# Post-norm decoder: who forms the norms' epsilon, bias and rows, and the masked queries

## The reference

```python
m = mean(x); v = var(x)                       # _layernorm
x = (x - m) / sqrt(v + 1e-5)

x = ln(x + nystrom_attention(x))              # 16 heads, 64 landmarks, 6 pseudo-inverse steps
x = ln(x + dilated_attention(x, ctx, ctx))    # 16 heads, three branches, causal
x = ln(x + ternary_ffn(x))                    # 256 -> 1024 -> 256, gelu
x = ln(x + memory_attention(x))               # 4 heads, decayed and causal
x = ln(x + gated_attention(x, ctx, ctx))      # 8 heads, rope; has a norm of its own inside
x = ln(x + experts(x))                        # 8 experts, top 2
```

## Time and profile before

| | before |
|---|---|
| median of 3 runs | 1829.68 us (1816.7 to 1835.09) |
| the profiled execution's own time | 1817.69 us |
| its span | 1815.6 us |
| mean granted PE clock | 0.90 |
| PE busy | 1408.0 us, 78% |
| PE weight loads busy | 1161.9 us, 64% |
| DVE (VectorE) busy | 1055.8 us, 58% |
| ACT (ScalarE) busy | 628.7 us, 35% |
| POOL (GpSimd) busy | 370.1 us, 20% |

### The profile page before, as it was taken

The page is one execution under the profiler, slowest core; times in us unless marked ns, Lnnn a source line. Parts: engine busy times, 40 slices in busy tenths (PEclk is TensorE's granted clock), DMA queues, the critical chain, the costliest instruction groups (busy, mean ns, idle before and its releaser), DMA issues. The chain is left out here.

```text
span 1815.6 us, 46593 instructions
## 1 busy us (share of the span) xinstructions
PE 1408.0 (78%) x19740; PEld 1161.9 (64%) x19740; DVE 1055.8 (58%) x2385; ACT 628.7 (35%) x1371; POOL 370.1 (20%) x374
## 2 busy tenths in 40 slices
PE   1798886799788679988777988866405999999960
PEld 0696664479577359866546966644404888888860
DVE  4577568567666676766857675684132444444425
ACT  1322543432353434243443314533102434443420
POOL 0013132211314121211511121421342000000016
PEclk9798998989999799999888989989657999999985
DMA  6111122211211123100413201201244766677723
GB/s 262 37 50 36 49 58 79 74 49 38 59 29 44 49 76 107 44 13 2 116 53 100 62 25 49 82 1 42 68 147 142 254 221 217 216 235 243 228 76 119
DMA packets 165449, 174.80 MB, mean 96 GB/s; under 512 B 10528, under 2 KB 130208, under 8 KB 164896
## 3 DMA queue, kind: packets, MB, share of 16 engines
q1 hardware_dynamic: 154688, 154.33, 26.9%
q10 hardware_dynamic: 7520, 9.58, 1.5%
q0 software_dynamic: 3072, 8.39, 1.4%
HBM read 126.39 MB, written 45.88 MB: 95 GB/s over the span
## 5 line engine op out<-in xcount | busy, mean ns | idle before, releaser
L2092 PE MATMUL m_bank<-e_xT,e_w 128*128 128x256 bf16 x2208 | 246.2, 274 | 0.5 <-DVE e_xT L2170 0.5
L2092 PEld LDWEIGHTS m_bank<-e_xT,e_w 128*128 128x128 bf16 x2208 | 216.7, 98 | 26.7 <-DVE e_xT L2170 0.9
L684 PE MATMUL bank<-arena 64*64 64x64 f32 (+2 forms) x6400 | 219.0, 227 | 8.4 <-DVE arena L869 3.5
L684 PEld LDWEIGHTS bank<-arena 64*64 64x64 f32 x6400 | 213.5, 138 | 16.7 <-issue 6.2
L1724 POOL TENSOR_TENSOR e_parts<-e_whole,e_parts 128x512 bf16<-128x512 f32 x96 | 112.6, 1178 | 512.0 <-ACT e_parts L1718 512.0
L2183 DVE TENSOR_TENSOR e_h<-m_bank,e_silu 128x256 f32<-128x256 f32 x184 | 78.2, 425 | 202.6 <-ACT e_silu L2135 202.6
L2104 PE MATMUL m_bank<-m_xT,e_h 128*128 128x256 bf16 x1104 | 124.1, 273 | 0.0
L2104 PEld LDWEIGHTS m_bank<-m_xT,e_h 128*128 128x128 bf16 x1104 | 108.0, 98 | 12.3
L2135 ACT ACTIVATE e_silu<-m_bank 128x256 f32<-128x256 f32 x184 | 70.5, 383 | 124.8 <-PE m_bank L2092 124.8
L1541 DVE TENSOR_REDUCE arena<-bank 128x1 f32<-128x512 f32 x128 | 79.8, 683 | 28.7 <-PE bank L1452 28.4
L1609 ACT ACTIVATE arena<-bank 128x512 f32<-128x512 f32 x128 | 66.5, 604 | 82.9 <-PE bank L1477 82.8
(11 more groups left out here) (295 smaller groups left out, 2721.9 us busy)
## 6 DMA issues: line engine op xcount, KB each, us to landing
e_w<-parts SPq DMA_DIRECT2D x92, 512.0 KB, 5.4
e_whole<-E SPq DMA_DIRECT2D x96, 256.0 KB, 3.1
parts<-e_parts SPq DMA_DIRECT2D x192, 128.0 KB, 2.9
m_xT<-parts SPq DMA_DIRECT2D x46, 512.0 KB, 8.0
slots<-zeros SPq DMA_DIRECT2D x4, 1536.0 KB, 7.5
back<-e_y ACTq DMA_DIRECT2D x23, 256.0 KB, 6.5
e_x<-slots SPq DMA_DIRECT2D x22, 256.0 KB, 6.7
w_rest<-W_rest SPq DMA_DIRECT2D x1, 3584.0 KB, 25.0
```

What stands on the lines that cost most here:

```text
L684: last = pe.matmul(b[r, p * width:(p + 1) * width], lhs[r, 4 * g + p, :], rhs[r, 4 * g + p, :], start=True, stop=True)
L2092: last = pe.matmul(bank[b][:, col:col + SLOTS], w[:, wp, c, f * P:(f + 1) * P], xeT[u][:, xp, c, :], start=j == 0, stop=j == len(terms) - 1)
```

## The change

ScalarE writes the normalised rows, as an activation with a scale (the reciprocal standard deviation) and a bias; VectorE forms only that bias, −mean × rstd, two columns; GpSimd adds the epsilon ahead of the power. ScalarE also forms the masked queries, from a bias that the setup has multiplied by the parity once. The tables of all five engines' orders are written anew.

```diff
-        def dve_norm(dve, bat, link, key, src, dst):
+        def dve_norm(dve, bat, link, key, src):
...
             for t in range(NT):
                 last = dve.bn_aggr(v["mv"][:, t, :], v["st"][:, t, :])
-            link(last)
-            dve.tensor_scalar(v["ve"][:], v["mv"][:, :, 1], EPS, None, ALU.add).then_inc(sem(f"variance{key}_{s}"), 1)
+            last.then_inc(sem(f"variance{key}_{s}"), 1)
             yield
             dve.wait_ge(sem(f"rstd{key}_{s}"), due("rstd", bat, 1))
+            dve.scalar_tensor_tensor(v["shift"][:], v["mv"][:, :, 0], -1.0, v["rstd"][:], ALU.mult, ALU.mult)\
+                .then_inc(sem(f"shift{key}_{s}"), 1)
+
+        def act_normalize(act, bat, key, src, dst):
+            s, v = bat % STREAMS, st[bat]
+            act.wait_ge(sem(f"shift{key}_{s}"), due("shift", bat, 1))
             for t in range(NT):
-                last = dve.tensor_scalar(dst[:, t, :], src[:, t, :], v["mv"][:, t, 0:1], v["rstd"][:, t:t + 1],
-                                         ALU.subtract, ALU.mult)
+                last = act.activation(dst[:, t, :], src[:, t, :], ACT.Identity, bias=v["shift"][:, t:t + 1],
+                                      scale=v["rstd"][:, t:t + 1])
             last.then_inc(sem(f"x{key}_{s}"), 1)
...
         def pool_norm(pool, bat, key):
             s, v = bat % STREAMS, st[bat]
             pool.wait_ge(sem(f"variance{key}_{s}"), due("variance", bat, 1))
+            pool.tensor_tensor(out=v["ve"][:], in0=v["mv"][:, :, 1], in1=EPSC[:], op=ALU.add).then_inc(sem(f"above{key}_{s}"), 1)
+            pool.wait_ge(sem(f"above{key}_{s}"), due("variance", bat, 1))
             pool.tensor_tensor(out=v["rstd"][:], in0=v["ve"][:], in1=NEGH[:], op=ALU.pow)\
                 .then_inc(sem(f"rstd{key}_{s}"), 1)
...
+                for u in range(2):
+                    link(dve.tensor_scalar(dq_masked[:, NC * u:NC * (u + 1)], bias["dq"], consts["parity"][:, u:u + 1], None, ALU.mult))
...
-            b = bk.await_filled(dve, "d_q")
+            b = bk.await_filled(act, "d_q")
             for u in range(2):
                 for m in range(NC):
-                    last = dve.tensor_scalar(n["qm"][:, u, m, :], b[:, m * T:(m + 1) * T], bias["dq"][:, m:m + 1],
-                                             consts["parity"][:, u:u + 1], ALU.add, ALU.mult)
+                    last = act.activation(n["qm"][:, u, m, :], b[:, m * T:(m + 1) * T], ACT.Identity,
+                                          bias=dq_masked[:, 2 * u + m:2 * u + m + 1], scale=consts["parity"][:, u:u + 1])
             last.then_inc(bk.emptied("d_q"), 1)
...
 ORDERS = {
-    "pe": """0x2 1x2 0x1 1x2 0x1 1x1 0x1 1x2 0x2 1x2 0x1 1x1 0x1 1x8 0x1 1x6 0x8 1x5 0x18 1x24 0x12 1x7 0x2 1x32 0x1 1x7 0x9 1x2
+    "pe": """1x2 0x2 1x2 0x1 1x1 0x2 1x2 0x2 1x2 0x1 1x1 0x1 1x8 0x1 1x5 0x2 1x25 0x6 1x4 0x23 1x40 0x3 1x2 0x13 1x6 0x3 1x1 0x12
```

More of the change, by code:

```diff
@@ L188 @@
+    1x4 2x1 0x1 2x1 0x3 2x6 1x2 2x1 1x1 0x2 2x1 0x1 2x6 1x3 0x1 1x1 0x1 2x1 1x2 0x1 2x1 0x1 1x4 2x1 0x2 2x1 0x3 2x1 0x1
+    2x2 1x1 2x2 1x3 2x1 0x4 2x7 1x2 2x1 1x1 0x1 2x1 0x1 2x1 0x1 2x5 1x2 2x2 1x1 0x1 1x1 0x1 2x1 0x2 1x4 0x1 1x2 0x5 2x4
+    1x1 0x1 2x1 1x1 0x1""",
+    "sp": """2x24 3x2 2x21 1x3 0x3 2x24 1x2 2x3 0x2 2x9 3x1 2x39 1x2 2x2 0x2 2x19 1x2 2x3 3x1 2x3 0x2 2x48 1x1 2x2 1x1 2x4 0x2 2x3
+    3x1 2x12 1x2 2x3 0x2 2x70 1x1 0x1""",
 }
-PER_BATCH = {"input_turned": 16, "input": 16, "context": 16, "stored": 16, "res": 5, "variance": 1, "rstd": 1, "x": 1,
+PER_BATCH = {"input_turned": 16, "input": 16, "context": 16, "stored": 16, "res": 5, "variance": 1, "rstd": 1, "shift": 1, "x": 1,
@@ L451, in layers_kernel @@
         NEGH = sb("neghalf", [P, NT])
+        EPSC = sb("epsilon", [P, NT])
+        dq_masked = sb("dq_masked", [P, 2 * NC])
         with nc.Block() as block:
@@ L477, in _ @@
                 pool.memset(NEGH[:], -0.5)
+                pool.memset(EPSC[:], EPS)
                 pool.memset(zeros[:], 0.0)
@@ L941, in act_nystrom @@
             yield
+            act_normalize(act, bat, "0", v["y"], v["x"])
+            yield
             act_norm(act, bat, "n_xT")
@@ L983, in dve_residual_norm @@
             bk.await_emptied(dve, name)
-            yield from dve_norm(dve, bat, link, key, v["y"], v["x"])
+            yield from dve_norm(dve, bat, link, key, v["y"])
         def pool_norm(pool, bat, key):
@@ L1143, in dve_dilated @@
             yield
-            b = bk.await_filled(dve, "d_q")
-            for u in range(2):
-                for m in range(NC):
-                    last = dve.tensor_scalar(n["qm"][:, u, m, :], b[:, m * T:(m + 1) * T], bias["dq"][:, m:m + 1],
-                                             consts["parity"][:, u:u + 1], ALU.add, ALU.mult)
-            last.then_inc(bk.emptied("d_q"), 1)
-            yield
             b = bk.await_filled(dve, "d_v")
@@ L1227, in act_dilated @@
             yield
+            b = bk.await_filled(act, "d_q")
+            for u in range(2):
+                for m in range(NC):
+                    last = act.activation(n["qm"][:, u, m, :], b[:, m * T:(m + 1) * T], ACT.Identity,
+                                          bias=dq_masked[:, 2 * u + m:2 * u + m + 1], scale=consts["parity"][:, u:u + 1])
+            last.then_inc(bk.emptied("d_q"), 1)
+            yield
             b = bk.await_filled(act, "d_k")
@@ L1562, in dve_gated @@
             bk.await_emptied(dve, "g_out")
-            yield from dve_norm(dve, bat, link, "4", n["u"], n["n"])
+            yield from dve_norm(dve, bat, link, "4", n["u"])
             yield
@@ L1572, in dve_gated @@
             yield
-            yield from dve_norm(dve, bat, link, "5", v["y"], v["y"])
+            yield from dve_norm(dve, bat, link, "5", v["y"])
         def act_gated(act, bat):
@@ L1611, in act_gated @@
             yield
+            act_normalize(act, bat, "4", n["u"], n["n"])
+            yield
             b = bk.await_filled(act, "g_nT")
```

98 lines of the change are left out of this document (51 added, 47 removed).

## The result

The changed kernel takes **1863.97 us** (median of 4, 1862.84 to 1868.64) against 1826.76 us (median of 4, 1816.7 to 1835.09) for the kernel before: a ratio of 1.0211, interval 1.0154 to 1.0268. It is about 38 us slower. The prediction was 1820 us, with a range of 1792 to 1850; both are missed on the slow side.

The account below looks back on a forecast made before the run. No engine was taken as full: two streams of dependent steps fill each other's gaps, and PE's waits count. −15 + 20 − 13 + 4, say −4 us, from 1823.7, halfway between two scales, gave 1820 us, range 1792 to 1850.

Parts of the forecast that it names:

- VectorE's relief: Layers: net 60 us less work on VectorE, of which a quarter reaches the end, −15 us (−5 and −30 kept).
- the prediction named 75: Layers: sign that PE's waits for VectorE outside norms fall from 97 to about 75 us; if they stay, relief worthless.
- The chain: Each norm, from PE's product to PE's transposes: 0.9 us longer, between +0.6 and +1.3, from 3.6 to 4.5 us.
- the bound for the add: GpSimd's two-column epsilon add in each norm: 0.4 us taken, between a memset's 0.10 and the power's 0.78.
- What the chain costs: The 40 norms that feed PE: 53 us not covered by the other stream's work with chain 4.5, +20 us.
- What the order gives back: Waits at lines 1122 and 1294: the new order hides most of one (−9) and half the other (−4), −13 us.
- The two named waits: PE at line 1122 for line 1197 (10.8 us in 8) and at 1294 for 1336 (8.6 in 8).
- ScalarE, +4 us: Layers: ScalarE gains 128 instructions, 72 us, of which 6% counts, as PE waits for it 6% of the time.
- The norm's chain becomes the bound: Rival, chance 0.22: feed-forward norms and stream 0's fourth, second and third pair; +25 us, about 1848.
- over 65 us of waits for the normalised x: Sign at PE's transposes: waits above about 65 us in all decide for the rival of the norm's chain as bound.
- Relief passes through: Rival, chance 0.30: VectorE bounds where ropes, row maxima and norms of both streams meet; −26 us, about 1798.
- nothing moves: Rival, chance 0.08: the order keeps PE's gaps as they are and both effects stay off PE, 1824 us.

Follow-up runs that it names:

- The queries: Kernel before with its old order, only the masked queries moved from VectorE to ScalarE: 1830.27 us, 1.0014.
- the new placement: The changed kernel's instructions under the five order tables of the kernel before (the old order): 1858.13 us, 1.0197.
- the second power: Kernel before, old order and placements, with one more GpSimd power into a spare tile ahead of each norm's power: 1856.44 us, 1.0166.
- The rows alone: Kernel before, old order, only the normalised rows moved to ScalarE, VectorE forming the bias: 1845.63 us, 1.0112.
- load added there: Kernel before with two more VectorE 128x256 instructions into a spare tile behind each norm's normalising pair, 96 in all: 1888.31 us, 1.0342.
- the old placement: The instructions of the kernel before, on their old engines, under the changed kernel's five order tables: 1853.03 us, 1.0169.
- the added load: Kernel before plus spare 128x256 instructions: 48 on ScalarE behind copies of norms' transposes (1827.41 us, 0.9995); the hardware note means 96 on VectorE behind norms (1888.31 us, 1.0342).

## Why the prediction was wrong, point by point

The sum was −15 + 20 − 13 + 4 = −4 us, and the measurement is +38. Three steps failed: the relief of VectorE and the order's gift did not come, and the sum had no term for PE being busy longer at a lower clock.

**VectorE's relief, −15 us: about nothing.** The queries' 15 us gave 1.0014, and the new placement with 47 us less VectorE work (808 to 761) costs no less than the second power, which relieves nothing. (The rows alone cost 10 us less than the second power at the same chain, but their intervals overlap, and the new placement with more relief does not bear it out.) The step that failed is "I take a quarter" of the removed work. PE's waits for VectorE outside norms stayed at 95.6 in the old order; the prediction named 75 and said that if they stay, the relief was worth nothing. At the one place read closely, the removed work stood where PE was itself held, in order, before the late rows; that this holds for all of it is argued and not shown. That load added there costs 62 us does not make its removal worth as much.

**The chain, +0.9 us: +0.62 measured, just in the range of 0.6 to 1.3.** The epsilon add took 0.238 and not 0.4, the bias 0.28 and not 0.2, each normalising instruction 0.592 and not 0.56. That both ends of the bound for the add were "start-up and not elements" is not so for the power: on 128x4 it takes 1.10 us (the experts' norm, in both traces), on 128x2 0.78. In the final order the mean chain is 4.44 us, 1.0 longer. That this is near the 0.9 is luck: over a third of it comes with the new order, from the row maxima that now stand in front of the bias, which the sum did not have.

**What the chain costs, +20 us: of the right size as waiting in the old order, but half of the whole.** Scaled to 0.62 us the prediction's 20 us give 14; in the old order the waits at the norms grew by 17.0. But the stretch grew by 35 us, since PE was busy 21.5 us longer. In the new order the count itself failed: it gave 53 us of uncovered norms and the trace has 30.2, under the 35 at which the prediction called its chain term wrong. The order covers the norms better than was counted, and waits appear elsewhere. The missing busy time is the largest failed step: the prediction had the granted clock in its rows (0.92) and no term for it. Some 7 us of the 21.5 are the profiled execution before, which had 0.903 against its own median of 0.898 (0.005 at 14.6 us for 0.01).

**What the order gives back, −13 us: nothing.** The two named waits shrank by 13.4 us (19.4 to 6.0), as foreseen, and the norms' waits too. Yet the new order gains nothing on the old one with the new placement (1.0211 against 1.0197), and with the old placement it loses 1.0169: I counted what the order covers and not what it uncovers. In the old placement the gated and dilated products' waits for VectorE's row maxima grew from 13.9 to 26.5 us and from 1.9 to 15.5. No kernel here mends these two places alone, so that they are the whole price is not shown.

**ScalarE, +4 us: nothing that can be measured**, by the added load (0.9995), and by PE's waits for ScalarE outside norms, 71.3 us before and 69.5 after. A term of 4 us is below what these runs can tell.

**Rivals.** "The norm's chain becomes the bound" came nearest, with 1848, and held in substance; but its sign, over 65 us of waits for the normalised x, did not appear (30.2). The waits moved to other lines, and the clock did the rest. "Relief passes through" and "nothing moves" are both excluded by the time. Of the other signs, PE's waits for VectorE outside norms rose to 121.8 us where about 75 were forecast, and the layers' stretch grew by 47 us, past the 25 at which the forecast called itself wrong altogether.

## What to carry to other kernels

In a kernel of two interleaved streams, price a step in a chain by the number of its occurrences, not by the waits found in front of it: here 48 norms cost about 50 us for each microsecond, about half of it waiting. Work taken off an engine counts only if PE can use the earlier result; look at what PE stands before at that moment. And where PE's granted clock is under 1, carry a term for it: here each microsecond of new waiting came with one or more of slower matmuls.

## What was new about the hardware

- VectorE instructions on 128x256 in SBUF took 0.40 us when GpSimd was idle and 1.01 in the mean, up to 2.5, when GpSimd's residual rows or memsets ran beside them (32 and 64 instructions of the added load).
- GpSimd's add of two columns takes 238 ns and its power 704 in the changed kernel (782 before). Two more columns cost the power about 0.32 us (1.10 on 128x4, against 0.78).
- The run-to-run spread of 1.3% of one kernel goes mostly with the granted clock: off the line of 14.6 us for each 0.01, the 83 times scatter by 2.0 us (standard deviation).
